# First attention: the router's roots on VectorE, row transfers without roots, dense pieces in the last pair

## What is computed

```python
x = x + attn_a(layernorm(x))                # softmax(q k^T / sqrt(128)) v, w_o
x = x + ffn(layernorm(x))
x = x + attn_b(layernorm(x))
x = x + ffn(layernorm(x))

def ffn(x):                                 # x: 4096 rows
    gates = softmax(x @ router_w)           # 8 experts
    idx1 = argmax(gates); idx2 = argmax(gates without idx1)
    pos1, pos2 = place of the row in its expert's list (cumulative sums), capacity 1280
    expert_in[e, place] = x[row]
    y = g1 * expert(expert_in)[...] + g2 * expert(...)[...]      # w1, silu, w2
    return y + 0.1 * (silu(x @ sw1 + sb1) @ sw2 + sb2)
```

## Time and profile before

| | |
|---|---|
| median of 3 runs | 773.42 us (767.63 to 775.83) |
| the profiled execution | 770.89 us, span of its instructions 769.1 us |
| granted TensorE clock, mean | 0.977 of full |
| first attention | 0 to about 100 us |
| first mixture | about 100 to 300 us |

### The profile page before, as it was taken

The page is one execution under the profiler, slowest core; times in us unless marked ns, Lnnn a source line. Parts: engine busy times, 40 slices in busy tenths (PEclk is TensorE's granted clock), DMA queues, the critical chain, the costliest instruction groups (busy, mean ns, idle before and its releaser), DMA issues.

```text
span 769.1 us, 18168 instructions
## 1 busy us (share of the span) xinstructions
PE 704.7 (92%) x6152; PEld 641.6 (83%) x6152; DVE 523.9 (68%) x1665; ACT 449.7 (58%) x1144; POOL 440.9 (57%) x564
## 2 busy tenths in 40 slices
PE   6888789799999997889999998999999899999996
PEld 5777689799999996667777776777779899999996
DVE  5877765366556565768888988877676556655536
ACT  2565454344444443677878878787755444456545
POOL 6367777166666651344545767777777265666640
PEclk9999869999999998899999999999999999999999
DMA  7997111455556334333533434333201346555328
GB/s 245 309 323 183 46 48 55 58 113 108 108 99 133 78 104 118 104 99 109 142 101 91 126 119 147 100 95 111 62 30 53 53 84 131 109 97 112 90 68 287
DMA packets 167715, 89.35 MB, mean 116 GB/s; under 512 B 120576, under 2 KB 151890, under 8 KB 167528
## 3 DMA queue, kind: packets, MB, share of 16 engines
q1 hardware_dynamic: 155704, 69.89, 36.6%
q0 software_dynamic: 9216, 17.34, 6.6%
q10 hardware_dynamic: 2704, 0.98, 0.6%
HBM read 49.63 MB, written 39.67 MB: 116 GB/s over the span
## 4 chain that ended last, share of the span: by engine, by line
PE 57%; DVE 5%; POOL 5%; DMA 5%; SPq 4%; issue 4%; ACT 3%; ACTq 0%; DVEq 0%; POOLq 0%
PE bank L940 22%; PE bank L919 19%; PE bank L1021 4%; DMA qc<-qk_rows 3%; SPq L439 3%; POOL x_slots L611 3%; PE bank L980 2%; PE bank L998 2%; PE bank L1002 2%; POOL pt L695 2%; DVE negp L1951 1%; PE bank L976 1%; PE bank L981 1%; ACT pt L1389 1%; PE bank L1040 1%
## 5 line engine op out<-in xcount | busy, mean ns | idle before, releaser
L1291 ACT ACTIVATE hT<-bank,bias_T 128x256 f32<-128x256 f32 x448 | 175.7, 476 | 186.4 <-PE bank L919 186.3
L626 POOL DMA_INDIRECT y_rows<-yo,row_cur x160 | 158.5, 990 | 127.9 <-DVE yo L1845 103.2
L1951 DVE TENSOR_REDUCE negp<-bank 128x2 f32<-128x512 f32 (+1 forms) x192 | 129.6, 685 | 44.3 <-PE bank L981 27.1
L940 PE MATMUL bank<-w_s,hT 128*128 128x128 f32 x1280 | 155.9, 275 | 0.0
L611 POOL DMA_INDIRECT x_slots<-xr,slot_u x128 | 129.9, 1015 | 38.7 <-issue 35.5
L940 PEld LDWEIGHTS bank<-w_s,hT 128*128 128x128 f32 x1280 | 150.0, 192 | 0.0
L919 PE MATMUL bank<-xT_hl,w_hl 128*128 128x256 f32 x960 | 135.4, 291 | 9.1 <-DVE xT_hl L1719 9.1
L695 POOL TENSOR_SCALAR_AFFINE_SELECT pt<-pt 128x512 f32<-128x512 f32 x128 | 86.0, 680 | 92.7 <-ACT pt L1389 92.2
L1389 ACT ACTIVATE pt<-bank 128x512 f32<-128x512 f32 x192 | 107.8, 596 | 40.3 <-PE bank L1002 38.5
L919 PEld LDWEIGHTS bank<-xT_hl,w_hl 128*128 128x128 f32 x960 | 120.9, 192 | 9.6 <-issue 9.6
L1845 DVE TENSOR_TENSOR yo<-bank,b_b 128x256 f32<-128x256 f32 x80 | 33.9, 424 | 98.7 <-PE bank L940 98.7
(11 more groups left out here) (214 smaller groups left out, 1194.0 us busy)
## 6 DMA issues: line engine op xcount, KB each, us to landing
xg_all<-x_slots SPq DMA_DIRECT2D x316, 32.0 KB
w_s<-in_L_ffn_w SPq DMA_DIRECT2D x32, 256.0 KB
qk_rows<-qks SPq DMA_DIRECT2D x16, 512.0 KB, 3.6
bdk<-qk_rows SPq DMA_DIRECT2D x187, 32.0 KB
qc<-qk_rows SPq DMA_DIRECT2D x45, 128.0 KB, 2.8
x_slots<-xg_all SPq DMA_DIRECT2D x1, 5440.0 KB, 21.7
y_rows<-xg_all SPq DMA_DIRECT2D x1, 4096.0 KB, 14.3
yab<-y_rows SPq DMA_DIRECT2D x16, 256.0 KB, 3.3
```

Of the source, the lines that this page charges most:

```text
L626: pool.indirect_dma_start(y_rows, bass.IndirectOffsetOnAxis(ap=row_cur[:, g % ROWS, j:j + 1], axis=0), yo[:, g % RING, j, :], None, bounds ...
L940: m = pe.matmul(yb(w, l)[:, j * P:(j + 1) * P], hT[:, w % 2, f, j * P:(j + 1) * P], wt[:, f, :], start=(f == 0), stop=(f == FT - 1))
L1291: a = act.activation(hT[:, w % 2, f, :], HB[2 * (w % 2) + f // 2][:, (f % 2) * 256:(f % 2) * 256 + 256], ACT.Silu, bias=bias_T[:, b0 + f:b ...
L1951: dve.tensor_reduce(dst, AB[(g + k) % 2][:, :].rearrange("p (j k) -> p j k", j=heads), AX.X, ALU.max, negate=True).then_inc(S.amax_done, 1)
```

## The change

1. The router's reciprocal root of the first mixture goes from GpSimd to VectorE: `root_of(n, k)`, nine steps on 4 columns each (a first value from the bits of the number, then two refinements, each step waiting for the one before). Steps 0 to 4 stand between the last five of `second`, step 5 behind them, steps 6 to 8 around `add_attn` and the first step of `placed` in the next pair. The second mixture keeps GpSimd's.
2. GpSimd's list in the first attention is only the 64 transfers, with no waits on TensorE and no roots.
3. `maxes` of the odd sequence (n + 1) moves from the head of a pair into the pair before, as `maxes(n + 3)` between steps of the second choice; `add_attn(n + 1)` and the statistics move ahead of or between the first steps of `second`; the norms of the router's rows stand one step later among those of `placed`.
4. `split_sw1` moves from pair 6 to the end of pair 5, and in the last pair TensorE does first_mm(0, 0) ahead of the values of sequence 14 and first_mm(0, 1) ahead of the router's logits; `silus(0, 0)` stands on ScalarE between the router copy and the gate exponentials of quad 6.
5. Items 0 to 3 and the last quads' router steps are written out by hand for each engine (`attn_a_end`); the loop `moe(0, ...)` starts at item 4. Definitions of functions that move in the file without a change are left out below.

```diff
             def rstd2_of(n):
                 pool.wait_ge(S.ln2_mv, n)
-                if n > PAIRS + 1:
-
-                    pool.wait_ge(S.xn2_ready, n - 1)
+                pool.wait_ge(S.xn2_ready, n - 1)
                 pool.tensor_scalar(ve2[:, :], mv2[:, :, 1], EPS, 1.0, ALU.add, ALU.mult).then_inc(S.ln2_ve, 1)
-                pool.wait_ge(S.ln2_ve, n)
+                pool.wait_ge(S.ln2_ve, n - PAIRS)
                 pool.tensor_tensor(rstd2[:, :], ve2[:, :], neg_half[:, :], ALU.pow).then_inc(S.ln2_rstd, 1)
 
@@ -636,39 +638,9 @@
                 pool.wait_ge(S.ln_rstd, 2)
                 key_ones()
                 query_masks()
-                for q in range(2, 7):
+                for q in range(2, 8):
                     rstd_of(q, q + 1)
-                rstd2_of(1)
-                rstd_of(7, 8)
-                rstd2_of(2)
-                k = 0
-
...
-                for i in range(2, PAIRS):
-                    n = 2 * i
-                    if i > 2:
-                        pool.wait_ge(S.probs_tr, n + 1)
-                        row()
-                        pool.wait_ge(S.gv_done, min(n + 3, SEQS))
-                        row()
-                    pool.wait_ge(S.y_done, n + 1)
-                    row()
-                    pool.wait_ge(S.probs_tr, n + 2)
-                    row()
-                    pool.wait_ge(S.gv_done, min(n + 4, SEQS))
-                    row()
-                    pool.wait_ge(S.y_done, n + 2)
-                    row()
-                    if i > 2:
-                        row()
-                    rstd2_of(i + 1)
-
-                for k in range(k, 2 * NT):
+                for k in range(2 * NT):
                     dispatch(0, k)
@@ -859,6 +831,8 @@
                     a_probs_transpose(n)
                 if 0 <= n + 1 < SEQS:
                     a_scores(n + 1)
+                if i == PAIRS - 1:
+                    first_mm(0, 0)
                 if 0 <= n + 2 < SEQS:
                     a_project(n + 2)
@@ -874,6 +848,8 @@
                     a_scores(n + 2)
                 if valid(i - 1):
                     r_transpose(i - 1)
+                if i == PAIRS - 1:
+                    first_mm(0, 1)
                 if 0 <= n + 3 < SEQS:
                     a_project(n + 3)
                 if valid(i - 1):
...
+            def attn_a_end():
+
+                last = PAIRS - 1
+                second_mm(0, 0)
+                first_mm(0, 2)
+                pe.wait_ge(S.pT_ready, SEQS)
+                counts(last - 1, bank[5])
+                r_transpose(last)
+                second_mm(0, 1)
+                r_logits(last)
+                first_mm(0, 3)
+                second_mm(0, 2)
+                counts(last, bank[5])
@@ -1262,6 +1243,8 @@
                     p_copy(n + 1)
                 if valid(i - 1):
                     r_copy(i - 1)
+                if i == PAIRS - 1:
+                    silus(0, 0)
                 if 0 <= n + 3 < SEQS:
                     g_copy(n + 3)
                 if 0 <= n + 2 < SEQS:
@@ -1273,13 +1256,6 @@
@@ -1468,7 +1446,12 @@
                 silus(1, 2)
                 silus(1, 3)
 
-            moe(0, 0, ITEMS - 1)
+            silus(0, 1)
+            r_copy(PAIRS - 1)
+            silus(0, 2)
+            gate_exps(PAIRS - 1)
+            silus(0, 3)
+            moe(0, START, ITEMS - 1)
             act.wait_ge(S.init_b, 1)
             for i in range(-1, PAIRS):
                 attn_b_pair(i)
...
+            def root_of(n, k):
+
+                y, t = root_y[:, 0, :], root_t[:, 0, :]
+                if k == 0:
+                    dve.wait_ge(S.ln2_mv, n + 1)
+                    a = dve.tensor_scalar(ve2[:, :], mv2[:, :, 1], EPS, None, ALU.add)
+                else:
+                    dve.wait_ge(S.root, ROOT * n + k)
+                if k == 1:
+                    a = dve.tensor_scalar(y.bitcast(I32), ve2[:, :].bitcast(I32), -0.5, ROOT_BITS, ALU.mult, ALU.add)
+                elif k == 2:
+                    a = dve.tensor_tensor(t, ve2[:, :], y, ALU.mult)
+                elif k == 3:
+                    a = dve.tensor_tensor(root_t[:, 1, :], t, y, ALU.mult)
+                elif k == 4:
+                    a = dve.scalar_tensor_tensor(out=t, in0=root_t[:, 1, :], scalar=-10.0 / 3.0, in1=root_t[:, 1, :], op0=ALU.add, op1=ALU.mult)
+                elif k == 5:
+                    a = dve.scalar_tensor_tensor(out=root_y[:, 1, :], in0=t, scalar=5.0, in1=y, op0=ALU.add, op1=ALU.mult)
+                elif k == 6:
+                    a = dve.tensor_tensor(t, ve2[:, :], root_y[:, 1, :], ALU.mult)
+                elif k == 7:
+                    a = dve.scalar_tensor_tensor(out=root_t[:, 1, :], in0=t, scalar=-0.5 * 0.375 ** 3, in1=root_y[:, 1, :], op0=ALU.mult, op1=ALU.mult)
+                elif k == 8:
+                    a = dve.scalar_tensor_tensor(out=rstd2[:, :], in0=root_t[:, 1, :], scalar=0.5625, in1=root_y[:, 1, :], op0=ALU.add, op1=ALU.mult)
+                a.then_inc(S.root, 1)
+
             def norm_r(n, j):
@@ -1524,7 +1533,10 @@
                         dve.wait_ge(S.slots1, 512)
                         dve.wait_ge(S.slots2_even, 256)
                         dve.wait_ge(S.slots2_odd, 256)
-                    dve.wait_ge(S.ln2_rstd, n + 1)
+                    if n < PAIRS:
+                        dve.wait_ge(S.root, ROOT * (n + 1))
+                    else:
+                        dve.wait_ge(S.ln2_rstd, n - PAIRS + 1)
                 a = dve.tensor_scalar(xr[:, t, 0:D], x[:, t, :], mv2[:, j, 0:1], rstd2[:, j:j + 1], ALU.subtract, ALU.mult)
                 if j == 3:
                     a.then_inc(S.xn2_ready, 1)
@@ -1723,15 +1735,23 @@
                 routed, led = valid(i - 2), valid(i - 1)
                 if valid(i):
                     inverse_sums(n)
-                if 0 <= n + 1 < SEQS:
-                    maxes(n + 1)
+                if led:
+                    root_of(i - 1, 6)
                 if valid(i):
                     add_attn(n)
-                for j in range(PLACED):
+                if led:
+                    root_of(i - 1, 7)
+                if routed:
+                    placed(i - 2, 0, bank[2])
+                if led:
+                    root_of(i - 1, 8)
+                for j in range(1, PLACED):
                     if routed:
                         placed(i - 2, j, bank[2])
-                    if led and j < 4:
-                        norm_r(i - 1, j)
+                    if led:
+                        norm_r(i - 1, j - 1)
+                if i == PAIRS - 1:
+                    x_split(0, 1)
                 if i == 0:
                     stats(4, 5)
                 if i < 0:
@@ -1761,33 +1781,34 @@
                         norm(i + 2, i + 3, j)
                 if i == -1:
                     stats(3, 4)
+                if valid(i):
+                    add_attn(n + 1)
                 if led:
                     second(i - 1, 0)
-                    second(i - 1, 1)
                 if valid(i):
                     stats2(i, 0)
                 if led:
-                    second(i - 1, 2)
-                    second(i - 1, 3)
-                if i == PAIRS - 2:
-                    split_sw1()
-                if i == PAIRS - 1:
-                    x_split(0, 0)
-                    x_split(0, 1)
-                if valid(i):
-                    add_attn(n + 1)
-                if led:
-                    second(i - 1, 4)
+                    second(i - 1, 1)
                 if valid(i):
                     dve.wait_ge(S.attn_added, n + 2)
                     stats2(i, 1)
                 if led:
-                    second(i - 1, 5)
+                    second(i - 1, 2)
+                if 0 <= n + 3 < SEQS:
+                    maxes(n + 3)
                 if valid(i):
                     stats2_end(i)
-                if led:
-                    second(i - 1, 6)
-                    second(i - 1, 7)
+                for j in range(3, SECOND):
+                    if led:
+                        second(i - 1, j)
+                    if valid(i):
+                        root_of(i, j - 3)
+                if i == PAIRS - 3:
+                    split_sw1()
+                if i == PAIRS - 2:
+                    x_split(0, 0)
+                if valid(i):
+                    root_of(i, 5)
 
             for i in range(-2, PAIRS):
                 if i == -1:
...
+            def attn_a_end():
+                last = PAIRS - 1
+                for k in range(6, ROOT):
+                    root_of(last, k)
+                for j in range(4):
+                    norm_r(last, j)
+                x_split(0, 2)
+                for k in range(PLACED):
+                    placed(last - 1, k, bank[5])
+                bias_add(0, 0)
+                y_copy(0, 0)
+                for k in range(LEAD):
+                    lead(last, k)
+                x_split(0, 3)
```

(9 more changed lines are left out.)

70 lines of the change are left out of this document (21 added, 49 removed).

## The result

| | before | after |
|---|---|---|
| median of 20 runs, us | 772.38 (767.63 to 778.16) | 777.92 (775.20 to 782.53) |
| span of the profiled execution, us | 769.1 | 777.4 |
| mean granted clock of TensorE | 0.977 | 0.975 |

The ratio after to before is 1.0075, 95% interval 1.0055 to 1.0095: about 5.5 us lost. The forecast was 772.2 us, a gain of 1.2. The time lies inside the range and within 1% of before, but on the other side of it, and the cause of the loss stands in none of the rivals as they were put.

A forecast was written before the change was run, and what follows sets the result against it. TensorE was busiest, but GpSimd's row transfers delayed its entry into chunk 0, worth at most 6.9 us. Entry 2.4 us sooner less 1.2 for low clock gave 1.2 gained: 769.7 profiled, median 772.2, range 765.5 to 779.5.

The forecast's parts named there:

- The pair: First attention's loop: a pair, from one router start to the next, grows by 0.45 us from 10.15 to 10.6.
- The max costs nothing either way, it only moves: VectorE's loop: moving the max itself costs nothing; only its wait for scores, +0.2 us a pair, was counted.
- Rival 3: Loop: the chain of roots shows in full, 1 us more a pair; loss 4.8 us, 778.2; chance 0.20.
- Start and router start of pair 6: First router start moves from 34.60 to about 35.25; that of pair 6 from 85.77 to 89.3, 3.5 us late.
- Last pair and pieces: End of the first attention: piece 4 starts 33.3 us behind the router start of pair 6, at 122.6 against 118.13.
- the allowance of 1.2 us for one low stretch: TensorE's idle 3.1 us before the first piece: one piece at the low clock, 2.7 us instead of 1.5.
- They meet, so the hole goes: Entry into chunk 0: TensorE ready at 141.9, GpSimd at 141.8, so no hole; 2.4 us gained.
- 6.5 us: Chunk 0: landing, loading and splitting from the last row's end (136.48) to TensorE's start (142.99), kept as in before.
- (2): Loop: roots hide fully in the dependence gaps, pair stays 10.15 us; gain 5.6, 767.8; chance 0.20.
- (4): Last pair: TensorE's low clock holds through it, costing 2.5 us more; loss 1.3, 775; chance 0.12.
- (5): Last pair: each ScalarE table load holds it as long again, 1.3 us; loss 1.4, 775; chance 0.03.
- X: Time TensorE enters chunk 0, counted as if at full clock: 144.3 in before, 141.9 forecast ahead of the clock allowance.

The follow-up runs named there:

- e6: The changed kernel with the max of the odd sequence put back at the head of its pair; 775.28 us, ratio to before 1.0047.
- e3: The changed kernel with no dense pieces in the last pair, the end of the first attention ordered as before; 773.78 us, ratio to before 1.0033.
- e2: The kernel before, with SyncE issuing all loads of chunk 0 in the first mixture; 770.23 us, ratio to before 0.9997.
- e11: The kernel before with SyncE loading chunk 0, its split ahead of the copy of item 8, and 12 pieces ahead instead of 10; 773.32 us, ratio 1.0023.
- e8: e3 plus SyncE loading all of chunk 0 and its split ahead of the copy of item 8; 769.34 us, ratio to before 0.9966.
- e9: e8 with the max of the odd sequence back at the head of its pair; 767.68 us, ratio to before 0.9949.
- e1: The changed kernel with SyncE issuing all four block loads of chunk 0 in the first mixture; 776.30 us, ratio to before 1.0075.
- e7: e1 plus VectorE's split of chunk 0 ahead of the copy of item 8; 777.38 us, ratio to before 1.0076.
- e10: The changed kernel with ScalarE's Silus of item 0 behind the gate exponentials of quad 6; 777.52 us, ratio to before 1.0070.
- e12: The kernel before with SyncE loading all of chunk 0 and its split ahead of the copy of item 8; 772.16 us, ratio to before 1.0012.

## Why the prediction was wrong, step by step

**The pair.** Predicted 10.6 us, measured 10.89: the mechanism was right, its size was 0.45 where 0.74 came. By its own terms: nine root steps were put at 0.8 us, and the early max at 0.2. The max's wait was as predicted (0.31 between starts against 0.1). Of the 0.29 that are missing, 0.16 are the root's integer step, 0.37 us long in three of the loop's pairs where 0.15 was the nearest row; the rest is in steps that wait for each other with next to nothing in between, once the max has gone from there (steps 4 to 6 are 0.2 apart). "The max costs nothing either way, it only moves" was wrong: moved, it cost 0.50 (e6), of which 0.2 had been counted. Rival 3, with 1 us a pair more than the forecast, was further off on the other side (11.6).

**Start and router start of pair 6.** Predicted +3.5 (its terms add up to 3.6), measured +4.75: 0.75 at the first start (predicted 0.65), 2.64 for the four pairs (0.58, 0.63, 0.69 and 0.74, predicted 4 x 0.45), and 1.36 for the pair with the split (11.88 against 10.52), which was put at 0.45 + 1.07 - 0.37 = 1.15. The missing 1.25 us are nearly all the pairs'.

**Last pair and pieces.** Predicted piece 4 at +33.3 us behind that start, measured +35.4. The first piece (+5.4, measured +5.55) was right. Up to the last router row the lateness was 1.0 us: the values behind the piece took 1.91 us at a lowered clock instead of 1.14, and the probabilities' transposes 1.10 instead of 0.60; the allowance of 1.2 us for one low stretch was for that. Up to the logits of quad 7 another microsecond came: about 0.3 on the way to the third piece, the rest behind it, where transposes and the second output piece still ran low (0.66 over 115.7 to 119.1). The walk was sound; the allowance covered one low stretch, and there were two. What the walk already contained, and the forecast didn't weigh, is that pieces in the last pair make it longer than before's (33.3 against 32.4) rather than shorter. e3 says it outright: without them the same distance is 31.7, and the second chunk comes 4.25 us sooner. (Before's own distance was 30.9 in e2 and e11, so 3.0 us may be less than the whole cost.) The pieces were taken as given in every rival; "leave them out" was the case that mattered.

**The step that failed: "They meet, so the hole goes".** TensorE's own time was put at 141.9 and was 145.2 (125.92 + 6 x 3.22), the two terms above. GpSimd's was put at 141.8, with 6.5 us from the end of the last row to the entry as in before. In after the last row ended at 139.14, 3.8 us later than forecast (quad 6 was placed 3.1 us later, and 16 rows took 21.2 us for 20.5), and the entry was 9.2 us behind it. With 6.5 us the two would have met again, at 145.2 and 145.6; the hole was there all the same. The 6.5 us were read as a length of landing, loading and splitting that moves with the rows; it is one only as long as the issuers are idle when the rows end. With TensorE and GpSimd meeting, ScalarE was not: its two loads stand behind Silus of piece 9, so the entry comes 1.9 us (Silus, first load) + 0.4 (second load) + 2.4 (its data) + 1.6 (splitting, the start of the matmuls) behind the start of piece 9, some 6.2 us, which is 3.0 more than a beat, whether the last row was out 3.0 us ahead of piece 9 (142.15 to 148.37 here) or 5.4 us (137.96 to 144.16 in e3). And since the low level came behind the hole (4.76 us from the entry to the second chunk, for a beat of 3.22), 4.7 us of the 6.9 remained. The sum, in the forecast's own form: +4.75 (router start) + 3.04 (last pair, piece 4) - 2.20 (hole) = +5.59, against 3.5 + 0.9 + 1.2 (the clock's allowance) - 6.9 = -1.3 in the forecast, which gave -1.2. Of the 6.9 us between the two sums the hole is 4.7, the router start 1.25 and the last pair 0.94. ("Seven blocks of root" among GpSimd's rows was a misreading, there are six; no term used it.)

That the hole would go with that order mended is shown by e8 and e9; that the order alone is enough is not: in e1 and e7, with the rows ready at 139.1, the entry was still 2.1 us behind "own", because the loads landed slowly. The cause of that is open.

**The rivals.** (2) is out: no run had a pair of 10.15 with roots on VectorE. (3) has the sign and 778.2 for 777.9, which is luck, for it has not the mechanism: its pair would have been 11.6 us, and the loss comes from three places. (4) the clock did not stay low through the last pair; the low stretches were two short ones, as the forecast had it, but in e10 they were longer. (5) a table load takes 1.29 us to the activation behind it in after too (103.33 to 104.62, 106.21 to 107.51), so it is out. By the Trainium skill, "ScalarE: Activation LUTs", section "What ACT_TABLE_LOAD costs", a drain of about 1.38 us would follow; neither kernel's trace shows it.

**What would have been seen.** Before had it. Its ScalarE starts the Silus of piece 9 1.7 us behind the piece (134.33):

```profile
136.04 1.57 ACT L1291 ACTIVATE hT<-bank,bias_T 128x256 f32<-128x256 f32 x4 [1.64 <-PE bank L919]
```

ScalarE's two loads stand behind them in its order (0.88 us for both issues at 138.07); from the last load's issue to the data it was 2.4 us (139.03), from there to the matmuls 1.6. Asking of each of the issuers of a chunk-0 load, when does it get to that instruction if the rows are sooner, would have given that floor. With the forecast's own times piece 9 starts at 141.9 - 3.2 = 138.7, the entry, 6.2 us on, is at 144.9, and with 1.5 us of low clock X is 146.4 against 144.3: a loss of 2.1 us, 3.3 with the allowance, before the pair and the last pair are corrected.

## What to carry to other kernels

A delay read between two events (last row to entry, 6.5 us) is only a constant while whoever issues in between is idle; when the first event is to move sooner, walk each issuer's own order again, and expect the wait to have a second owner. Work put into an engine's idle time in the middle of a chain is not free if it waits for something itself: what stands behind it on that engine waits too (3.9 us here for 3 us of matmuls). And moving an operation on a busy engine is not free because it is done anyway: the max, moved to where it waits for its scores and away from small steps that wait for each other, cost 0.34 us a pair.

## What the runs showed of the chip that was not expected

- A 4-column step on VectorE (L1511) has two lengths, and which one depends on where it falls beside GpSimd's row transfer (0.97 us busy). Started 0.60 us into a row it took 0.37, 0.37 and 0.36 us and ended with the row, in all three such pairs (61.42, 72.30, 83.20); started 0.36 us into one (50.63), between two (94.31, 109.49), or with none in flight (39.90) it took 0.17. e1, e3 and e7 repeat this. A norm of the router rows (L1540) takes 0.47 or 0.48 when it starts 0.55 us into a row, 0.27 to 0.34 otherwise. In the same part of a row a reciprocal (73.44) and a product of two tiles (73.56) kept their 0.16 us. e6 and e9 have the same loop: in e6 no norm of the pair was lengthened and it took 10.39 us; in e9 a row came to lie so that the last norm started 0.44 us into it and took 0.58, and that pair took 10.74. VectorE and GpSimd of e9:

```profile
73.32 0.58 DVE L1537 TENSOR_SCALAR xr<-x,mv,rstd 128x128 f32<-128x128 f32 x1
```

```profile
72.88 0.97 POOL L613 DMA_INDIRECT x_slots<-xr,slot_u  x1 [0.31 <-issue]
```

That the transfer is the cause fits all these rows and was not tried by itself.
- Short holes bring the low level of TensorE's clock too: behind an idle time of 1.86 us in e1 and 1.85 in e7 the second chunk came 4.8 us after the first instead of 3.22 (granted clock 0.63 from 147.4 to 152.0 in e1), so a hole of 1.9 us cost 3.4. Behind the 1.25 us in e9 the clock stayed full.
- The same load of chunk 0 took 1.87 us from issue to data in e12 and 3.46 in e7. Why is open.
